# Perceiver kernel: norms around the self-attention pair by pair, normalised on ScalarE, with transposes and gate products moved ahead

## The reference, cut to what matters

```python
x = x + retention(_layernorm(x))
xf = _layernorm(x)
y1 = _ln(xf + _mha(xf, in_proj_w, in_proj_b, out_proj_w, out_proj_b), ln1_g, ln1_b)
gates = softmax(y1 @ wg); idx = argmax(gates)     # one of 8 experts per row, capacity 128
y2 = _ln(y1 + moe(y1), ln2_g, ln2_b)
x = x + y2
```

## Time and profile before

| | |
|---|---|
| runs | 1460.54, 1464.1, 1466.36 us; median 1464.1 |
| profiled execution | 1461.73 us, span 1459.9 us, mean granted clock of TensorE 0.953 |
| busy share | TensorE 92%, VectorE 69%, ScalarE 44%, GpSimd 47% |

### The profile page before, as it was taken

One profiled execution on the slowest core, in us unless ns is written; L12 is line 12 of the kernel. 1 busy time (PEld: TensorE's weight loads), 2 busy tenths in 40 slices (PEclk: granted clock), 3 DMA queues, 4 the chain that ended last, 5 costly groups with the idle time before them and its releaser, 6 DMA issues. The chain is left out here.

```text
span 1459.9 us, 29132 instructions
## 1 busy us (share of the span) xinstructions
PE 1345.1 (92%) x11170; PEld 1091.7 (75%) x11170; DVE 1000.7 (69%) x2021; ACT 648.8 (44%) x1235; POOL 690.6 (47%) x592
## 2 busy tenths in 40 slices
PE   7899877689789999999999999999999997889998
PEld 4556555579768888888888888888888866557787
DVE  6999744445756777877787777877776666454454
ACT  3555314300164555555555554555555533333322
POOL 0142011300345877887688678766976544231100
PEclk9999999789899999999999999999999977889999
DMA  9998253007256877797779777878775560220000
GB/s 356 422 384 310 85 198 135 1 4 249 94 139 179 234 192 178 199 239 191 177 202 235 192 181 197 221 182 193 192 189 114 126 161 1 80 115 0 1 0 30
DMA packets 107575, 240.11 MB, mean 164 GB/s; under 512 B 30218, under 2 KB 76634, under 8 KB 104746
## 3 DMA queue, kind: packets, MB, share of 16 engines
q1 hardware_dynamic: 89070, 216.75, 52.4%
q10 hardware_dynamic: 18368, 21.50, 4.3%
HBM read 152.96 MB, written 6.40 MB: 109 GB/s over the span
## 5 line engine op out<-in xcount | busy, mean ns | idle before, releaser
L2495 DVE TENSOR_REDUCE d_top<-psum 128x1 f32<-128x400 f32 (+2 forms) x512 | 285.8, 573 | 80.7 <-PE psum L2044 72.1
L1935 POOL TENSOR_TENSOR d_ring<-d_ring 128x512 f32<-128x512 f32 x224 | 288.2, 1287 | 72.9 <-ACT d_ring L2283 55.1
L2283 ACT ACTIVATE d_ring<-psum 128x512 f32<-128x512 f32 (+1 forms) x416 | 229.6, 594 | 172.9 <-PE psum L2062 126.6
L2062 PEld LDWEIGHTS psum<-d_queries,d_stack 100*128 100x128 f32 (+1 forms) x1664 | 208.7, 191 | 42.5 <-issue 24.7
L2062 PE MATMUL psum<-d_queries,d_stack 100*128 100x128 f32 (+1 forms) x1664 | 227.8, 278 | 11.1 <-DVE d_queries L2510 5.9
L2044 PE MATMUL psum<-d_stack,d_queries 96*128 96x400 f32 (+1 forms) x512 | 203.3, 400 | 5.9 <-DVE d_top L2495 5.2
L2028 PE MATMUL psum<-d_wv,d_rowsT 128*128 128x256 f32 (+1 forms) x1248 | 207.4, 283 | 0.0
L2028 PEld LDWEIGHTS psum<-d_wv,d_rowsT 128*128 128x128 f32 (+1 forms) x1248 | 193.2, 187 | 1.9 <-issue 0.5
L1872 POOL TENSOR_TENSOR d_rowsT<-shared,d_rowsT 128x768 fp32r<-128x768 f32 (+2 forms) x62 | 118.5, 1913 | 148.1 <-ACT d_rowsT L2254 148.1
L2018 PE MATMUL psum<-d_rowsT,d_wk 128*128 128x384 f32 (+2 forms) x768 | 159.6, 357 | 11.7 <-DVE d_bv L2657 7.3
L2018 PEld LDWEIGHTS psum<-d_rowsT,d_wk 128*128 128x128 f32 x768 | 134.2, 194 | 23.1 <-DVE d_bv L2657 7.4
(11 more groups left out here) (432 smaller groups left out, 2167.6 us busy)
## 6 DMA issues: line engine op xcount, KB each, us to landing
d_stack<-d_stage SPq DMA_DIRECT2D x384, 200.2 KB, 4.2
a_cT<-ctxT_dram SPq DMA_DIRECT2D x14, 1601.0 KB, 14.2
a_cR<-ctx_rows_dram ACTq DMA_DIRECT2D x12, 1664.0 KB, 10.9
shared<-moe_w_dram SPq DMA_DIRECT2D x16, 1024.0 KB, 10.2
shared<-row_stds_dram SPq DMA_DIRECT2D x16, 801.0 KB, 6.7
shared<-ctxT_dram SPq DMA_DIRECT2D x32, 384.0 KB, 6.9
shared<-ctx_rows_dram SPq DMA_DIRECT2D x12, 896.0 KB, 6.2
shared<-ctx_rows_dram SPq DMA_DIRECT2D x12, 768.0 KB, 5.6
```

What stands on the lines that cost most here:

```text
L1935: pool.tensor_tensor(sums[:, 0, m, :], first, ring[:, slot_of(u, m, c), :], ALU.add)\
L2062: last = pe.matmul(ps[0:w, S_BANK + (m + c) % 2, j * P:(j + 1) * P], stack[0:STACKED, m, j, c * P:c * P + w], queries[0:STACKED, m, j, :], ...
L2283: act.activation(ring[0:w, slot_of(u, m, c), :], ps[0:w, S_BANK + (m + c) % 2, :], ACT.Exp)\
L2495: dve.tensor_reduce(top[:, m, v:v + 1], ps[:, M_BANK + v % 2, 0:min(w, S - s0)], X, ALU.max)\
```

## The change

A set of tensors (`Carried`) is allocated from the other end of SBUF, at the start of the retention, and freed between the two halves of the encoder block: the parameters `pb1`, statistics, the normalised rows `xf` and their transpose `xfT`.

1. SP issues the load of `pb1` as the first thing in the retention phase, and no longer in the self-attention phase, where nobody waits for it now.
2. The norm ahead of the self-attention is in the retention phase, pair by pair: after each addition to x VectorE takes the pair's moments and variance, ScalarE its root, VectorE the inverse and a shift of minus mean over deviation (one pair later), and ScalarE writes the two normalised tiles with scale and shift. TensorE transposes four tiles at a time, ScalarE and VectorE copy them out, all still in the retention phase. Self-attention starts with its projections.
3. The norm behind the self-attention goes in the same way, into `xf`. Gain and shift are put into the transposed copy by feature (from a small table of columns, which VectorE makes at the start of the phase), and into the rows by two two-input instructions per pair (`gained`), pairs 0 and 1 on GpSimd, 2 and 3 on VectorE.
4. Transposes and gate products of y1 are at the end of the self-attention phase, and the logits are in PSUM bank 0 instead of 4.

```diff
+def carried_moments(carried, dve, sig, tag, src, i):
+    pair = slice(2 * i, 2 * i + 2)
+    moments_of(dve, sig, tag, (carried.stats, carried.moments), src, range(2 * i, 2 * i + 2))
+    dve.wait_ge(sig(f"{tag}_moments"), 2 * i + 2)
+    dve.tensor_scalar(carried.var[:, pair], carried.moments[:, pair, 1], EPS, None, ALU.add).then_inc(sig(f"{tag}_var"), 1)
+def carried_root(carried, act, sig, tag, i):
+    act.wait_ge(sig(f"{tag}_var"), i + 1)
+    act.activation(carried.std[:, pair], carried.var[:, pair], ACT.Sqrt).then_inc(sig(f"{tag}_std"), 1)
+def carried_inverse(carried, dve, sig, tag, i):
+    dve.wait_ge(sig(f"{tag}_std"), i + 1)
+    dve.reciprocal(carried.rstd[:, pair], carried.std[:, pair]).then_inc(sig(f"{tag}_rstd"), 1)
+    dve.wait_ge(sig(f"{tag}_rstd"), i + 1)
+    dve.scalar_tensor_tensor(carried.shift[:, pair], carried.moments[:, pair, 0], -1.0, carried.rstd[:, pair],
+                             ALU.mult, ALU.mult).then_inc(sig(f"{tag}_shift"), 1)
+def carried_rows(carried, act, sig, tag, src, i):
+    act.wait_ge(sig(f"{tag}_shift"), i + 1)
+    for t in range(2 * i, 2 * i + 2):
+        act.activation(carried.xf[:, t, :], src[:, t, :], ACT.Identity, bias=carried.shift[:, t:t + 1],
+                       scale=carried.rstd[:, t:t + 1]).then_inc(sig(f"{tag}_out"), 1)
...
 def phase_retention
         def _(sp):
+            sp.dma_start(carried.params[:, :], drams["pb1"]).then_inc(sig("b_carried_in"), 16)
...
         def _(pe):
+            turn_tensor(pe, core, "b_next", carried.xf, 0, [(sig("b_next_out"), True)])
...
         def _(act):
+            for i in range(NT // 2):
+                carried_root(carried, act, sig, "b_next", i)
+                if i:
+                    carried_rows(carried, act, sig, "b_next", x, i - 1)
+            carried_rows(carried, act, sig, "b_next", x, NT // 2 - 1)
+            turn_scalar(act, core, "b_next", carried.xfT, 0, group=True)
...
         def _(dve):
             for i in range(NT // 2):
...
+                carried_moments(carried, dve, sig, "b_next", x, i)
+                if i:
+                    carried_inverse(carried, dve, sig, "b_next", i - 1)
+            carried_inverse(carried, dve, sig, "b_next", NT // 2 - 1)
+            turn_vector(dve, core, "b_next", carried.xfT, 0, group=True)
...
 def phase_mha
+        def gained(eng, i, tag, done):
+            pair = slice(2 * i, 2 * i + 2)
+            eng.wait_ge(sig("m_hat_out"), 2 * i + 2)
+            eng.tensor_tensor(y1[:, pair, :], xf[:, pair, :], core.p("ln1_g").unsqueeze(1).broadcast_to([P, 2, D]),
+                              ALU.mult).then_inc(sig(tag), 1)
...
+            eng.tensor_tensor(y1[:, pair, :], y1[:, pair, :], core.p("ln1_b").unsqueeze(1).broadcast_to([P, 2, D]),
+                              ALU.add).then_inc(sig(tag), 1)
         def _(sp):
-            sp.dma_start(params[:, :], drams["pb1"]).then_inc(sig("m_params_in"), 16)
...
         def _(pool):
+            for i in range(2):
+                gained(pool, i, "m_gained_p", i)
...
         def _(pe):
-            turn_tensor(pe, core, "m_xfT", xf, 0, [(sig("m_ln_out"), True)])
...
+            turn_hats(0)
+            pe.wait_ge(sig("c_params_in"), 16)
+            pe.wait_ge(sig("m_res"), 1)
+            logits(0)
+            turn_hats(1)
+            logits(1).then_inc(sig("c_logit_ps"), 1)
...
         def _(act):
-            norm_scalar(act, sig, "m_ln2", scratch2)
+            carried_root(carried, act, sig, "m_hat", 0)
+            carried_root(carried, act, sig, "m_hat", 1)
+            carried_rows(carried, act, sig, "m_hat", y1, 0)
+            carried_root(carried, act, sig, "m_hat", 2)
+            carried_rows(carried, act, sig, "m_hat", y1, 1)
+            turn(0, 0)
+            turn(1, 0)
+            carried_root(carried, act, sig, "m_hat", 3)
+            carried_rows(carried, act, sig, "m_hat", y1, 2)
+            carried_rows(carried, act, sig, "m_hat", y1, 3)
+            turn(0, 1)
...
         def _(dve):
+                carried_moments(carried, dve, sig, "m_hat", y1, i)
+                if i:
+                    carried_inverse(carried, dve, sig, "m_hat", i - 1)
+            carried_inverse(carried, dve, sig, "m_hat", NT // 2 - 1)
+            gained(dve, 2, "m_gained_d", 0)
+            dve.wait_ge(sig("c_y1T_ps"), 4)
+            dve.tensor_scalar(y1T[:, 1, HALF:N], ps[:, 7, :], columns[:, 1:2], columns[:, 3:4],
+                              ALU.mult, ALU.add).then_inc(sig("c_y1T_d"), 1)
+            gained(dve, 3, "m_gained_d", 1)
-            gained_norm(dve, sig, "m_ln2", scratch2, y1, y1, core.p("ln1_g"), lambda t: core.p("ln1_b"))
```

More of the change, by code:

```diff
@@ L94, in __init__, with tensor @@
         self.params, self.packs = {}, {}
[L96 to L97 removed]
+    def tensor(self, ctx, name, shape, dt=F32, side="left"):
+        return ctx.enter_context(self.nc.sbuf_tensor(name, shape, dt, side=side))
     def phase(self, build, *args):
@@ L103, in phase, with load_pack @@
         self.sig.close()
-    def load_pack(self, ctx, pack):
-        tile = self.tensor(ctx, pack, [P, WIDTH[pack]])
+    def load_pack(self, ctx, pack, side="left"):
+        tile = self.tensor(ctx, pack, [P, WIDTH[pack]], side=side)
         self.packs[pack] = tile
@@ L248, in turn_vector, with project_tensor @@
         last.then_inc(core.sig(f"{tag}_d"), 1)
-def project_tensor(pe, core, tag, weight, src, first, src_tag, free=(), ready=(), order=(0, 1)):
+def project_tensor(pe, core, tag, weight, src, first, src_tag=None, free=(), ready=(), order=(0, 1)):
     for s, v in tuple(free) + tuple(ready):
@@ L1187, in _, with turn_hats, logits @@
             rows_tensor(pe, core, "m_proj", oT, core.w("mha_woT"), 0, both(sig, "m_oT", G) + [(sig("m_probT"), G)])
+            def turn_hats(c):
+                pe.wait_ge(sig("m_hat_out"), 4 * c + 4)
+                for k in range(KD):
+                    for j in range(4):
+                        last = pe.transpose(ps[:, 4 + 2 * c + k, j * P:(j + 1) * P], xf[:, 4 * c + j, k * P:(k + 1) * P],
+                                            core.p("ident"))
+                    last.then_inc(sig("c_y1T_ps"), 1)
+            def logits(c):
+                pe.wait_ge(sig("c_y1T_a"), 2 + c)
+                if c:
+                    pe.wait_ge(sig("c_y1T_d"), 1)
+                for t in range(4 * c, 4 * c + 4):
+                    for k in range(KD):
+                        last = pe.matmul(ps[:, 0, t * E:(t + 1) * E], y1T[:, k, t * P:(t + 1) * P],
+                                         core.w("moe_wg")[:, k, :], start=(k == 0), stop=(k == KD - 1))
+                return last
+            turn_hats(0)
[4 more added lines that the diff above has]
+            logits(1).then_inc(sig("c_logit_ps"), 1)
         @block.scalar
         def _(act):
-            norm_scalar(act, sig, "m_ln", scratch)
-            turn_scalar(act, core, "m_xfT", xfT, 0, group=True)
-            act.wait_ge(sig("m_params_in"), 16)
             project_scalar(act, core, "m_qT", qT, 4, core.p("mha_bq"))
@@ L1363, in _ @@
         def _(pe):
-            turn_tensor(pe, core, "c_y1T", y1, 0, [])
-            pe.wait_ge(sig("c_params_in"), 16)
-            for c in range(2):
-                for s, n in both(sig, "c_y1T", c + 1):
-                    pe.wait_ge(s, n)
-                for t in range(4 * c, 4 * c + 4):
-                    for k in range(KD):
-                        last = pe.matmul(ps[:, 4, t * E:(t + 1) * E], y1T[:, k, t * P:(t + 1) * P],
-                                         core.w("moe_wg")[:, k, :], start=(k == 0), stop=(k == KD - 1))
-            last.then_inc(sig("c_logit_ps"), 1)
             pe.wait_ge(sig("c_onehB"), 1)
```

75 lines of the change are left out of this document (45 added, 30 removed).

## The result

The changed kernel took 1470.8 us (median of 7 runs, 1467.91 to 1475.3), the kernel before beside it 1465.5 (7 runs): a ratio of 1.0045, 95% interval 1.0024 to 1.0066. A second series of 12 runs gave 1.0043 (1.0019 to 1.0068). The ratios are those on record for each series; the plain ratio of two medians differs from them by up to 0.0016, and here it is 1.0036. By the ratios the change costs 6.3 to 6.6 us (by the first medians alone 5.3), where the forecast had +3.4. The profiled execution took 1475.3 us, the slowest of its 7 runs; before it was 1461.73. The page of the changed kernel answers to the earlier trace rows: the span is 13.5 us longer, and TensorE is busy 15.6 us more with as many matmuls.

What follows compares the result with a forecast made beforehand. It took TensorE, busy 92% of the span, as the bound, so delay at the first dispatch matmul reaches the end. First seam +0.3 and second seam +3.1 gave +3.4 us on the 1464.1 us median: 1467.5 us, range 1458 to 1472.

Steps and rivals of the forecast that it cites:

- First seam, order of the work: Retention tail to projections: pairwise norm and transposes start projections 1.0 to 1.3 us sooner, taken as 1.3.
- First seam, clock loss: Projections of self-attention: TensorE's short waits leave them starting at clock 0.50, losing 1.6 us, bounds 0 to 3.
- Middle: Stages between the projections and the second seam: given no term, counted on only to shift.
- Tail: End of self-attention: expert block starts at 288.2 instead of 281.80, bounds 286 to 289, with logits in hand.
- The holds: Self-attention tail: GpSimd gain products of 1.28 us each hold VectorE's variance and shift of pairs 2 and 3.
- transposes at full clock (1.09 for eight): Self-attention tail: the first eight transposes take 1.09 us, ending at 277.9.
- I take 2.6: Self-attention tail: first sixteen gate products take 2.6 us, between 2.2 at full clock and 3.4 at low clock.
- Head: Start of expert block: GpSimd's 4.50 us addition holds VectorE, so first dispatch comes 12.2 us after block start, at 300.4.
- the named row: Expert head sign: a small VectorE slot instruction or place tile lasting over 3 us, ending with GpSimd's addition.
- VectorE gets in first: Expert head rival: slot products and place tile 0 pass before GpSimd's bias addition, giving 1464.2 us; chance 0.15.
- no hold to speak of: Second-seam rival: GpSimd does not hold VectorE, first dispatch at 293.1, giving 1460.2 us; chance 0.16.
- The clock stays low in the projections: First-seam rival: the 32 projection matmuls take 14 us more instead of 1.6, giving 1479.9 us; chance 0.04.

Runs made afterwards that it cites:

- second profile of the changed kernel: The changed kernel unaltered, run again beside the kernel before and profiled on the fastest of its 12 runs: 1473.2 us, ratio 1.0043.
- second seam only: Kernel before with only the new norm behind self-attention, GpSimd gain products, and transposes and gate products moved ahead; old first seam: 1470.1 us, ratio 1.0041.
- first seam alone: Changed kernel with its norm ahead of self-attention in the retention phase, but the old self-attention tail and expert head: 1465.8 us, ratio 1.0002.
- kernel with fillers in both seams: Changed kernel plus filler matmuls (outputs nobody reads) in the retention and self-attention tails, nothing moved: 1465.2 us, ratio 1.0000.
- gain products late: Changed kernel with GpSimd's gain products of pairs 0 and 1 waiting until all eight tiles are normalised: 1468.7 us, ratio 1.0027.
- Moving the addition: Changed kernel with GpSimd's shift addition to x waiting until VectorE has made all place and spread tiles: 1470.8 us, ratio 1.0032.
- kernel before with short fillers: Kernel before plus filler matmuls fitted to its waits: one behind the last retention output, six before the transposes, nine behind the output projection: 1464.6 us, ratio 1.0004.
- both late, fillers, tail: Changed kernel with GpSimd's shift addition and gain products both moved later, plus four filler matmuls in the self-attention tail: 1462.1 us, ratio 0.9992.
- all edits: Changed kernel with GpSimd's gain products and shift addition late, fillers in both tails and the expert-block head reordered: 1457.3 us, ratio 0.9945.

## Why the prediction was wrong

The direction and nearly every mechanism held, and the size did not: +3.4 us forecast, +6.3 to +6.6 measured by the ratios. By stages the forecast was +0.3 for the first seam, nothing for the middle, +6.4 for the tail and −3.3 for the head. The second profile of the changed kernel has +0.6, +0.5, +9.1 and −3.6, which makes +6.6. The step that failed is the clock in the tail, taken as full for the first transposes and nearly full for the first gate products. The forecast's bounds by stages add up to at most +5.6 us (1.7 + 0.8 + 3.1), 1469.7 us, though 1471 is written there; the loss by the ratios lies above that sum. By its own steps:

**First seam, order of the work: right.** A gain of 1.3 us up to the projections was taken, and 1.2 measured (15.03 to 13.85). Rows were taken at 0.50 us and took 0.59 less an overlap (1.09 for two); the last normalised tile came 10.1 us behind the first addition, predicted 10.2. The column table was held for 5.03 us by GpSimd and cost nothing, as said. The parameters were there in time.

**First seam, clock loss: about right.** Taken as 1.6 (0 to 3), measured 3.1 in the first profile of the changed kernel (17.03 against 13.97), just outside, and 1.7 in the second (15.71). The unchanged first seam lost 2.2 in the profile of the second seam only (16.22), so the kernel before had a good draw, and what the change itself adds is not shown. The seam's net of +0.3 was +0.6 in the second profile and +1.9 in the first. By time, the first seam alone is 1.0002.

**Middle: a step that was missing.** The prediction counted on the stages behind the projections to only shift. They took 0.5 to 2.1 us more, with 15.3 and 32.6 us at 0.50 where before it was 13.7. Of the other kernels without fillers the one with the old first seam (second seam only) had 13.7 again, the others 15.3 to 32.6. The kernel with fillers in both seams had 29.3, so a held clock at the seam does not secure it; what decides it stays open.

**Tail: the term that was mis-sized.** Block start was put at 288.2, which is 20.3 us behind the first residual addition (bounds 18.1 to 21.1); it came at 22.8. The holds were as described: variance 0.85, shift 1.23, pairs 2 and 3. The clock was not: the step "transposes at full clock (1.09 for eight)" measured 1.97, "I take 2.6" for the first gate products 3.55, the second transposes 1.95 for 1.75, the second gate products 3.56 for 3.4. That is 0.88 + 0.95 + 0.20 + 0.16 = 2.2 us of the 2.5. Another 0.8 lies ahead of the first transposes (9.7 us behind the first addition, predicted 8.9). It is there already when the first shift is done (4.7 us, predicted 3.8): the second addition started 2.53 us behind the first, where 1.8 was taken, after a wait of 0.63 for the output matmuls, of which the 32 took 9.81 us instead of 8.59. Smaller gaps give 0.5 back. The error of judgment is plain in the text: it quotes gate products at 0.50 for 7 us as evidence and then takes a value 0.85 us below half of them, in the hope that eight short transposes would keep the clock. In the windows the clock fell between 283 and 285, while TensorE waited and before the transposes began. Hold and clock are also tied together: with the gain products late the transposes began 1.6 us sooner and still found the clock at 1.00. The kernel with fillers in both tails, same holds, was 1.8 us shorter in this stage and 0.0043 faster in all.

The root's table load, which now waits for the first variance (277.31, 1.28 us), had no term. It lies beside the statistics of pair 1 and the reciprocal is not late by it, so it costs nothing.

**Head: right.** The price of 12.2 us from block start to dispatch was 11.8, with the named row (3.60 us ending with GpSimd's 4.50) and the named longest wait. Moving the addition shortened the head by 3.4 us.

**Rivals.** "VectorE gets in first" and "no hold to speak of" fell to the rows of 0.85 and 3.60 us. "The clock stays low in the projections", 14 us, fell too: at 219 it was back at 1.00. The true case lies between the forecast and that one: the clock is low for longer in the projections, in the middle and in the tail, and costs a few tenths to 3 us in each.

The page cited in the prediction, the Trainium skill's SBUF — State Buffer, Who interferes with whom, agrees with the rows: a held VectorE instruction ends with the GpSimd instruction beside it, at 2, 8 and 64 columns alike (0.85, 3.60 and 2.66 us). By the Trainium skill's TensorE: Matmul & The Clock Gate, The HAM clock gate, sustained activity releases the clock; the prediction did not count on it. The rows go both ways: the same 32 gate products behind the same transposes stayed at 0.50 in the kernel before (6.9 us) and rose to 1.00 in the kernel with the first seam only (3.94 us).

## What to carry to other kernels

Work taken off a serial seam and cut into pairs leaves TensorE with several short waits in place of one long one, and what it does between them then runs at the low clock: price every piece behind a wait at the rate of the low rows. Before an engine is given "free" work beside a norm, list the small two-column instructions of the other that the chain needs; GpSimd's 1.3 and 4.5 us instructions here made the tail 2.1 us and the head 3.4 us longer through instructions of 0.17. A filler costs little in a true wait and a lot beside it (0.86 us each, 7 us in all when too many), and it pays only once the order of the work lets the time saved through: in the old head GpSimd's addition took what the clock gave. A seam's time in one profile is one draw of the clock; look at a second profile, or at a kernel in which that seam is unchanged, before a loss of 2 us is given a cause.

## What the runs showed of the hardware beyond the expectation

The same gate products, back to back and with TensorE busy all of the time, ran at either level of the clock and changed it in either direction. In the kernel before they stayed at 0.50 for all of their 6.9 us. In the kernel before with short fillers they began at 1.00, behind fillers and transposes at 1.00, and fell to 0.50 while they ran. In the kernel with the first seam only, which has the old head and no fillers, they began at 0.50, behind transposes at 0.50, and were at 1.00 from 291.3 on. The first two windows below are of the kernel with short fillers, the third is of the first seam only; the number behind the length is busy TensorE, and the granted clock is third from the end:

```profile
285.30:286.30 1.00, 1.00 (x9) 1.00 (x10) 0.78 (x3) 0.98 (x4) 1.00 (x3) 0.92 0.00 0
286.50:288.00 1.50, 1.50 (x8) 1.50 (x9) 0.00 (x0) 0.83 (x1) 1.50 (x3) 0.50 0.00 0
...
291.30:293.50 2.20, 2.20 (x20) 2.11 (x19) 0.22 (x1) 0.03 (x1) 2.20 (x3) 1.00 0.00 0
```

Why it went one way in one profile and the other way in another is not shown. Cut into two halves with a wide filler ahead of each, the same 32 took 1.95 and 1.92 us at 1.00 in the tails of two kernels (both late, fillers, tail; all edits), but in the changed kernel with fillers in both tails the second half took 3.42. Two engines that alternate on products with two SBUF inputs wait for each other in turn: GpSimd's took 1.5 to 1.7 us (1.26 alone) and VectorE's 1.6 (0.69 alone).
